# A graph attention kernel: a quad's gathers wait for VectorE's product and sums by head in place of parts of ScalarE's weighing

## The reference, cut to what matters

```python
h = relu(layernorm(x))
q, k, v = (h @ W.T + b per head, 8 heads of 32)
sim  = einsum('hed,hed->eh', q[:, dst], k[:, src]) / sqrt(32)
p    = exp(sim - segment_max(sim, dst))          # edges are sorted by dst
attn = p / segment_sum(p, dst)
out  = x + segment_sum(attn * v[:, src], dst) @ Wo.T + bo
```

## Time and profile before

| | |
|---|---|
| median of 3 runs | 6950.24 us (6938.55 to 6957.0) |
| the profiled execution's own time | 6949.4 us |
| its span in the trace | 6947.6 us |
| busy over the span | PE 4531.6, DVE 4539.1, ACT 3956.7, POOL 4638.8 us |
| gathers of the attention loop | 1760, from 3740.3 to 6691.5 us |

### The profile page before, as it was taken

How to read it: one execution, slowest core, us unless ns; L and a number is a source line. 1 busy time by engine, 2 the same in 40 slices (tenths; PEclk the granted TensorE clock), 3 DMA queues, 4 the chain that set the end, 5 groups by cost and what they waited for, 6 DMA issues and landing times. The chain is left out here.

```text
span 6947.6 us, 117508 instructions
## 1 busy us (share of the span) xinstructions
PE 4531.6 (65%) x19717; PEld 3355.2 (48%) x19717; DVE 4539.1 (65%) x12295; ACT 3956.7 (57%) x14482; POOL 4638.8 (67%) x3716
## 2 busy tenths in 40 slices
PE   1366666666666666664886677777677777777767
PEld 1344444444444545543553555555555555555545
DVE  4565555555556666663554777777777777777766
ACT  0665555555555555552332667677676767677661
POOL 1478888888888888887554566666666666666630
PEclk6677777777777777776998888888888888788889
DMA  8767777777777777778774566666666666676746
GB/s 314 188 105 106 104 107 106 106 107 106 106 106 109 107 109 107 110 108 184 263 260 144 167 183 190 188 195 187 199 190 198 197 196 201 199 206 202 206 145 196
DMA packets 644181, 1130.07 MB, mean 163 GB/s; under 512 B 74529, under 2 KB 466795, under 8 KB 643445
## 3 DMA queue, kind: packets, MB, share of 16 engines
q0 software_dynamic: 367600, 678.97, 49.7%
q1 hardware_dynamic: 223985, 273.78, 12.1%
q10 hardware_dynamic: 51860, 169.74, 7.4%
HBM read 929.80 MB, written 451.51 MB: 199 GB/s over the span
## 5 line engine op out<-in xcount | busy, mean ns | idle before, releaser
L701 POOL DMA_INDIRECT sums<-mtw,posIw x1563 | 2489.4, 1593 | 599.1 <-issue 408.2
L1249 POOL DMA_INDIRECT kv<-kvt,sI x1760 | 1763.8, 1002 | 1044.0 <-ACT room L1613 654.3
L1613 ACT ACTIVATE room<-kv,pp 128x33 f32<-128x33 f32 x8800 | 1918.1, 308 | 42.3 <-issue 38.1
L1528 PE MATMUL ps<-room,Of 128*128 128x264 f32 x3520 | 1143.0, 467 | 611.5 <-issue 339.3
L734 PE MATMUL ps<-h,wf 128*128 x3320 | 1212.0, 518 | 303.3 <-DVE mtw L825 230.6
L718 PE MATMUL ps<-Mw,Oh 128*128 128x128 f32 x3320 | 672.7, 368 | 926.9 <-DVE Oh L852 926.9
L825 DVE SCALAR_TENSOR_TENSOR mtw<-mtw,cont,ps 128x256 f32 x1660 | 794.2, 478 | 619.2 <-SPq L690 452.1
L1528 PEld LDWEIGHTS ps<-room,Of 128*128 128x128 f32 x3520 | 727.3, 224 | 890.7 <-issue 618.2
L718 PEld LDWEIGHTS ps<-Mw,Oh 128*128 128x128 f32 x3320 | 630.1, 274 | 1041.7 <-DVE Oh L852 1011.7
L734 PEld LDWEIGHTS ps<-h,wf 128*128 128x128 f32 x3320 | 805.8, 260 | 590.8 <-issue 455.3
L799 ACT COPY wf<-ps 128x512 f32<-128x512 f32 x415 | 242.7, 585 | 1238.8 <-PE ps L718 870.3
(11 more groups left out here) (223 smaller groups left out, 4509.3 us busy)
## 6 DMA issues: line engine op xcount, KB each, us to landing
qb<-qt SPq DMA_DIRECT2D x880, 192.0 KB
accd<-acc SPq DMA_DIRECT2D x880, 132.0 KB
ints<-srows ACTq DMA_DIRECT2D x205, 512.0 KB
OT<-drows SPq DMA_DIRECT2D x110, 512.0 KB
sums<-zero ACTq DMA_DIRECT2D x72, 704.0 KB
part<-sums SPq DMA_DIRECT2D x56, 896.0 KB
kv<-kvt,sI POOLq DMA_INDIRECT x1760
kvt<-kvo SPq DMA_DIRECT2D x98, 260.0 KB
```

The costliest lines, as they stand in the source:

```text
L701: e.indirect_dma_start(sums[t % NS], bass.IndirectOffsetOnAxis(ap=posI[:, t % NP:t % NP + 1], axis=0), mt[:, t % NM, :], None, compute_op= ...
L1249: e.indirect_dma_start(kv[:, s % NK, :], None, kvt, bass.IndirectOffsetOnAxis(ap=sI[:, s:s + 1], axis=0)).then_inc(kvs.sem(s), 16)
L1528: m = e.matmul(psum[6 + j % 2][:, 0:NH * 33], lhsT=Of[:, w % 2, k % W2, :], rhs=pv[:, k % NV, :], start=(k % 2 == 0), stop=(k % 2 == 1))
L1613: e.activation(pv[:, s % NV, h * 33:h * 33 + 33], kv[:, s % NK, D + h * 33:D + h * 33 + 33], ACT.Copy, scale=pp[:, w % 2, h, s % W2:s % W2 ...
```

## The change: what it does

It concerns the waits of GpSimd ahead of the gathers of quads 11 and later, 429 of 440. The waits of the second, third and fourth gather for a part of `l_wact` go. In their place the first waits for `l_prod` at g-2, that is the product of quad g-3, and the third for `l_red` at g-2, the sums by head of quad g-3. The wait ahead of the first gather for quad g-11 stays. No instruction of any engine is added, dropped or moved apart from the waits, and the gathers are issued in the same order.

```diff
                         if g >= NK // 4:
                             wait_weighed(e, g - NK // 4)
                         for s in range(max(NE, 4 * g), 4 * g + 4):
-                            if g >= NK // 4 and s % 4:
-                                before = NH * weighed(1, g - NK // 4)
-                                e.wait_ge(S("l_wact"), before + s % 4 * NH * len(shares(g - NK // 4 + 1)[1]) // 4)
+                            if g >= NK // 4 and s % 4 == 0:
+                                e.wait_ge(S("l_prod"), g - 2)
+                            if g >= NK // 4 and s % 4 == 2:
+                                e.wait_ge(S("l_red"), g - 2)
                             gather(e, s)
```

## The result

| | before | after |
|---|---|---|
| median | 6951.26 us (6938.55 to 6957.0, 4 runs) | 7142.08 us (7128.8 to 7153.32, 4 runs) |
| ratio | | 1.0276, 95% interval 1.0252 to 1.0301 |
| the profiled execution, its span | 6949.4, 6947.6 us | 7128.8, 7126.2 us |

The change costs 191 us, 2.8%. The forecast was 137 us more, 7086 in a range of 6850 to 7170.

What follows compares the result with a forecast made beforehand. No engine is full; late updates of TensorE and ScalarE, lagging during unbroken gathers, set the time. Extension 1.85 less regain 0.57 gives 1.28 us per window, over 107 windows +137 us: 7086 us, range 6850 to 7170.

Steps and rivals of the forecast that it cites:

- first kind of window: Windows with `tops` late: the run of gathers ends one gather later, so `tops` starts 1.25 us later.
- the lower of the two values in the prediction: Windows with `lim` late: run ends 3.75 us later, or 2.50 where the second gather was not held; 2.50 was taken.
- some 2.7 us after the run's last gather: Late updates of TensorE and ScalarE arrive about 2.7 us after the start of the last gather in a run.
- The term of the extension: Longer gather runs delay `tops` by 1.25 us and `lim` by 2.50, weighed by 39 and 36 waits: 1.85 us per window.
- `lim` by 2 us more: Sign of being right: `tops` and `lim` still late in nearly every window, `lim` by 2 us more than now.
- The term of the regain: After the stall GpSimd is held less by ScalarE, so the next long run starts 0.57 us earlier per window.
- waits for ScalarE fall to under 2 us per window: Sign of being right: GpSimd's waits for ScalarE fall from 6 us per window to under 2.
- rival C: New waits hardly bind; no change, 6949 us, only if the ring's wait for quad g-11 holds gathers; 0.15 with another rival.
- The new waits at nothing: Gathers' waits for VectorE's product and sums cost nil, being mostly met already where GpSimd is behind.
- The meeting of `columns` and GpSimd's weighing: One more such meeting per window on the path would add 0.42 x 107 = 45 us; nothing was added.
- A: Rival: every window becomes of the shorter kind, `tops` never late, -139 us, 6810 us; chance 0.27.
- B: Rival: ScalarE's 80 updates per window cause the lateness; `lim` comes about 8 us after `spread` regardless; 6930 to 6949; 0.15 shared.

Runs made afterwards that it cites:

- e1: The kernel before without its waits for parts of ScalarE's weighing and without the new waits for VectorE: 7126.5 us, ratio 1.0254.
- e12: The changed kernel again, unchanged, on another chip of the slower kind, against the kernel before: 7166.45 us, ratio 1.0305.
- e4: The kernel before with one update of `l_wact` per weighed slot in place of eight, gathers' waits by whole slots: 7047.54 us, ratio 1.0146.
- e13: The kernel before with gathers held for copies `tops` and `lim` in place of parts of ScalarE's weighing, slower kind of chip: 6984.13 us, ratio 1.004.
- e8: The kernel before with gathers held for copies `tops` and `lim` in place of parts of ScalarE's weighing, faster kind of chip: 6380.56 us, ratio 1.0003.
- e3: The changed kernel with both new waits one quad nearer (g-1), against the kernel before on a faster chip: 6498.64 us, ratio 1.0185.

## Why the prediction was right, and where its sizes were off

*Direction and mechanism.* The step that carried it holds: the removed waits are what ends a run of gathers, and without them the late updates come later. e1 shows that the removal does nearly all of it, and the counts of held gathers show the runs go on to a quad's end. In the first kind of window the run grew by the one gather forecast. In the second it grew by two where it reached the quad's end, as the lower of the two values in the prediction has it (three in the window shown). That the updates come some 2.7 us after the run's last gather holds for `tops`, in 24 of 36 cases between 2.5 and 3.1 us, and worse for `lim` and `pp`: in 15 of 34 and 27 of 28 cases they did not wait for the run's end.

*The term of the extension, 1.85 us per window.* It was that `tops` and `lim` wait longer. In the changed kernel they wait 427.8 us in 68.0 windows, 6.3 us, against 400.3 in 71.8, 5.6 us: 0.7 us more and not 1.85. The mark "`lim` by 2 us more" failed: it was 0.6 us. Instead `pp`, not in the sum at all, waits 1.7 us more (124.8 us in 68.0 windows against 10.2 in 71.8), and VectorE's `add` gives back 0.7 (106.2 us in 68.0 windows against 162.9 in 71.8). 0.7 + 1.7 - 0.7 = 1.7 us; these waits overlap, so that this is no account, only a size. In e1, the removal alone, the term is met nearly as it was worked out: `tops` and `lim` wait 504.5 us in 67.3 windows (1076 gathers), 7.5 us, 1.9 more than before. So the 1.85 us is right for the removal, and that the loss in the changed kernel has the same size while `pp` makes the largest part of it is in part luck.

*The term of the regain, 0.57 us.* It is the one that failed in the total. Measured is 191 / 107 = 1.78 us per window by the medians, and 1.5 in the stretch from 4500 to 6400 us (27.9 against 26.5), where the sum gave 1.28. GpSimd was thought to be less held by ScalarE afterwards. It is held as much, 6.0 us per window against 6.1, because the ring's wait for quad g-11, which the change leaves, now meets the same late or delayed weighing (5.49 and 6.94 us in the rows above). The mark "waits for ScalarE fall to under 2 us per window" was wrong for the same reason; they fall so only in number. I gave this wait no place in the sum, only in the text of rival C.

*The new waits at nothing.* Right in time, to 0.5% (e1, e12); they do shift which update is late. *The meeting of `columns` and GpSimd's weighing:* no run bears on it.

*The rivals.* A did not come: `tops` is late as often as before. B's cause fell with e4, and its sign, a `lim` as soon after `spread` as before, did not show in e1 (9.3 us at the median, 7.8 before); in the changed kernel it nearly did (8.1 us). C, as a change without effect, did not come. VectorE's updates were indeed enough for GpSimd: nearly all its waits are for ScalarE or for nothing.

*What the forecast rested on unseen.* It was right on a chip of one kind. On the other kind a window of a like kernel takes 21.5 us, the gathers go on without a break and nothing is late. So "while gathers are issued without a break, updates of TensorE and ScalarE lag" holds on one kind of chip and not on the other; the trace of before could not tell that the lateness belongs to a chip, or to the state that it is in.

## What to carry to other kernels

A wait that looks like idle time ahead of a transfer may be the brake that lets other engines' updates through: before it is taken out, ask what happens to everything else in the time in which the transfers then run on. Where a copy waits and its matmul has long been done, look at what the whole core does when it is let go, not at its maker. A brake taken from one engine moves the jam to the next due update, so count all of a loop's updates and not the two that wait longest. And measure on more than one chip before you put down a mechanism: here the same kernel took 6.95 ms on some and 6.38 ms on others, and the jam was on the first alone.

## What the runs showed of the hardware that was not expected

- On chips of the slower kind updates of TensorE and ScalarE reached the waiting engine late: up to 9.6 us after the instruction had ended in the windows shown, at the median 7.6 us (`tops`) and 7.8 us (`lim`) in the kernel before, and 12.2 us at most (a `lim` in e12). None of the late `tops` and `lim` before came more than 3.1 us after the start of the last gather ahead of it. No row shows it of VectorE's. The ends of matmuls are modelled in the profile, so for TensorE it could be the matmul that is late; ScalarE's last weighing in the earlier trace rows ended at 5510.15 by its record, and GpSimd's gather was let go at 5513.62.
- The time of arrival can be moved by moving the gathers' pauses (the change, e1, e13). But it is no property of gathers alone: in e8 they ran without a break for 1500 us and nothing was late.
- The lateness was there in three groups of runs (the kernel before at 6948 to 6956 us, on at least two chips) and not in two others (6379 and 6381 us) with the same programs. One kernel shows both: 6984.13 and 6380.56 us, windows of 26.6 (1143 gathers in 1900 us) and 21.5 us. The whole difference lies in the attention loop: its first gather starts at 3735.2 us in the one and 3742.7 in the other, behind 1563 indirect transfers of GpSimd in the first layer. In the loop TensorE's granted clock was 0.94 to 0.96 where gathers ran and nothing was late (e3, e8) and 0.82 to 0.85 where updates were late (before, after, e12, e13); whether that is a cause or comes of TensorE's being busier is not shown. Whether it is the chip, or something set on it at the time, is open. Both groups without it held kernels without gathers, too, and that cannot be told apart either.
- With nothing late, little can be won on the gathers: with a plain transfer in their place the kernel is 2.4 and 2.5% faster, with none at all 1.6 and 1.7%. Why none is not the faster of the two, no run shows.
